# One-hots of slots laid out block by block in a two-stage mixture-of-experts kernel, and a second product taken by chunk halves

## What is computed

```python
x = x + _L0_ffn_ref(_L0_cond_ref(x, cond_8, ...), router_w, w1, b1, w2, b2)   # top 2 of 8 experts per token
x = x + _L1_ffn_ref(_L1_cond_ref(x, cond_8, ...), Wg, W1, b1, W2, b2)         # each expert takes its top 256 tokens
# _L1_ffn_ref:
G, I = jax.lax.top_k(S, k)                     # S: experts x tokens, k = 256
hid = gelu(einsum('ekh,ehf->ekf', xt[I], W1) + b1[:, None, :])
out = (einsum('ekf,efh->ekh', hid, W2) + b2[:, None, :]) * G[..., None]
new_x = zeros.at[I.reshape(-1)].add(out.reshape(-1, h))
```

## Time and profile before

| | before |
|---|---|
| median of 3 runs | 155.68 us (155.34 to 156.07) |
| span of the profiled execution | 153.7 us |
| median less span | 1.98 us |
| TensorE busy | 141.9 us (92%), 1100 matmuls |
| VectorE busy | 92.6 us (60%), 306 instructions |
| ScalarE busy | 82.2 us (53%) |
| GpSimd busy | 57.3 us (37%) |
| mean granted TensorE clock | 0.997 |

### The profile page before, as it was taken

How to read it: one execution, slowest core, us unless ns; L and a number is a source line. 1 busy time by engine, 2 the same in 40 slices (tenths; PEclk the granted TensorE clock), 3 DMA queues, 4 the chain that set the end, 5 groups by cost and what they waited for, 6 DMA issues and landing times.

```text
span 153.7 us, 3561 instructions
## 1 busy us (share of the span) xinstructions
PE 141.9 (92%) x1100; PEld 123.3 (80%) x1100; DVE 92.6 (60%) x306; ACT 82.2 (53%) x247; POOL 57.3 (37%) x62
## 2 busy tenths in 40 slices
PE   7999698899999999999799997979997999999990
PEld 3847687799999999964689975748986888889990
DVE  0278957756655555450599777765531685754872
ACT  0596807667777765620367769985126344445000
POOL 0000277344477554461500000002677777773000
PEclk9999999999999999999999999999999999999998
DMA  5994517999999972112702940040122221656634
GB/s 155 346 407 164 138 42 227 383 345 343 402 389 341 294 254 96 34 55 84 209 0 110 394 184 0 4 145 2 28 44 59 56 55 52 188 179 183 191 87 136
DMA packets 19252, 26.15 MB, mean 170 GB/s; under 512 B 1970, under 2 KB 13618, under 8 KB 18850
## 3 DMA queue, kind: packets, MB, share of 16 engines
q1 hardware_dynamic: 16386, 21.73, 41.6%
q0 software_dynamic: 1760, 3.67, 8.0%
q10 hardware_dynamic: 1088, 0.52, 1.2%
HBM read 19.98 MB, written 5.93 MB: 169 GB/s over the span
## 4 chain that ended last, share of the span: by engine, by line
PE 68%; DVE 15%; issue 5%; DMA 4%; POOL 4%; DVEq 1%; ACT 1%; POOLq 0%
PE bank L573 12%; PE bank L583 12%; PE bank L741 11%; PE bank L652 10%; PE bank L751 5%; POOL xg L445 3%; PE bank L475 3%; PE bank L619 3%; PE bank L628 2%; DMA xg<-rows,idx 2%; DVE y L1050 2%; DMA picked<-y,sidx 1%; DMA got<-picked 1%; DVE hid L1145 1%; PE bank L498 1%
## 5 line engine op out<-in xcount | busy, mean ns | idle before, releaser
L849 ACT ACTIVATE hT<-bank,w_now 128x128 f32<-128x128 f32 x92 | 26.3, 368 | 12.9 <-PE bank L573 12.9
L573 PE MATMUL bank<-xg,w_now 128*128 (+1 forms) x184 | 24.7, 277 | 1.3 <-ACT xg L842 0.8
L423 POOL DMA_INDIRECT xs<-rows,gidx x15 | 14.6, 976 | 28.6 <-DVE gidx L1057 17.9
L926 ACT ACTIVATE h1T<-bank,c_sb 128x256 f32<-128x256 f32 x44 | 18.2, 473 | 12.5 <-PE bank L652 12.5
L583 PE MATMUL bank<-w_sb,hT 128*128 (+1 forms) x184 | 24.4, 276 | 0.3 <-ACT hT L849 0.3
L573 PEld LDWEIGHTS bank<-xg,w_now 128*128 128x128 f32 x184 | 22.4, 192 | 2.4 <-issue 1.8
L583 PEld LDWEIGHTS bank<-w_sb,hT 128*128 128x128 f32 x184 | 22.4, 192 | 0.5 <-ACT hT L849 0.5
L741 PE MATMUL bank<-v_sb,h1T 128*128 128x128 f32 x176 | 22.7, 280 | 0.0
L741 PEld LDWEIGHTS bank<-v_sb,h1T 128*128 128x128 f32 x176 | 20.9, 192 | 1.4 <-ACT h1T L926 1.2
L428 POOL DMA_INDIRECT picked<-y,sidx x16 | 15.6, 977 | 10.3 <-DVE y L1106 9.1
L445 POOL DMA_INDIRECT xg<-rows,idx x14 | 14.0, 1000 | 5.7 <-issue 3.4
(11 more groups left out here) (201 smaller groups left out, 231.5 us busy)
## 6 DMA issues: line engine op xcount, KB each, us to landing
v_sb<-in_v SPq DMA_DIRECT2D x16, 256.0 KB
cw_sb<-in_cond_w SPq DMA_DIRECT2D x8, 386.5 KB, 5.4
plane<-y SPq DMA_DIRECT2D x5, 512.0 KB, 5.5
w_sb<-plane SPq DMA_DIRECT2D x5, 512.0 KB, 5.1
w_sb<-in_w SPq DMA_DIRECT2D x2, 1024.0 KB, 8.3
w_sb<-in_w SPq DMA_DIRECT2D x1, 1290.0 KB, 7.0
w_sb<-in_w SPq DMA_DIRECT2D x1, 774.0 KB, 4.9
rows<-row SPq DMA_DIRECT2D x1, 544.0 KB, 3.4
```

Source lines behind the costliest of these rows:

```text
L423: pool.indirect_dma_start(out=xs[:, b % RING], out_offset=None, in_=rows0, in_offset=rows_at(gidx, b)).then_inc(gathered[b % RING], 16)
L573: mm = pe.matmul(bank[2 + j % 2][:, P * f:P * f + P], w1_now[:, j % WB_RING, P * f:P * f + P], xsT[:, bass.ds((j - e) * P, P)], start=True ...
L849: ins = act.activation(hT[:, j % 2, P * f:P * f + P], bank[2 + j % 2][:, P * f:P * f + P], ACT.Relu, bias=w1_now[:, j % WB_RING, F + f:F + ...
L926: act.activation(h1T[:, n % 2, fc], bank[UP_BANKS[(2 * n + h) % 4]][:, CAP * f:CAP * f + CAP], ACT.Gelu, bias=c1_sb[:, e * NF + fc:e * NF ...
```

## The change

The one-hots of both stages are laid out block by block, `slot1h[i, s]` with the place s fastest. Each is made by one `tensor_scalar` compare per block of 128 tokens: the row of column numbers `iota` (128 bf16) against one float32 value per partition, read from a copy of the places (`locf`, `loc1f`). Stage one so has 16 compares of 128 elements in place of 2 of 1024, and each `place(e)` of stage two 8 in place of 1. `loc1` is now written in the order of its source. Both tables of repeated column numbers and the waits for them go. TensorE waits for the first-stage one-hots four at a time. A wait of VectorE for its own `hlf1h` is added ahead of `place`. For units 4 to 9 (six of the seven sparse experts) `down_e` gives way to `down_both`, which takes the hidden chunks 0 and 1 for both row halves first and then waits for the second half of the gelu and takes chunks 2 and 3; the last unit keeps `down_e`.

```diff
-        slot1h = sb("slot1h", [P, P, K * NC], BF16)
+        locf = sb("locf", [P, K * NC])
+        slot1h = sb("slot1h", [P, K * NC, P], BF16)
...
-        loc1 = sb("loc1", [P, E, NC], I16)
-
-        one1 = slot1h[:].rearrange("p s i -> p (s i)").rearrange("p (r s c) -> p r s c", r=2, c=NC)
+        loc1 = sb("loc1", [P, NC * E], I16)
+        loc1f = sb("loc1f", [P, NC, E])
+
+        one1 = slot1h[:].rearrange("p (r c) s -> p r c s", r=2)
...
             for i in range(K * NC):
-                pe.wait_ge(onehots, i // NC + 1)
-                mm = pe.matmul(bank[1][:, 0:2 * NB], slot1h[:, :, i], blkv[:, i].rearrange("p v b -> p (v b)"),
+                pe.wait_ge(onehots, i // 4 + 1)
+                mm = pe.matmul(bank[1][:, 0:2 * NB], slot1h[:, i], blkv[:, i].rearrange("p v b -> p (v b)"),
...
-                    mm = pe.matmul(bank[1][:, 0:2 * NH], one1[:, e % 2, :, c],
+                    mm = pe.matmul(bank[1][:, 0:2 * NH], one1[:, e % 2, c],
...
+            def down_both(n):
+                e = unit[n][1]
+                pe.wait_ge(h1T_ready, 4 * n + 2)
+                if n == HEAD:
+                    pe.wait_ge(yd_kept, HEAD)
+                if n == HEAD + 1:
+                    pe.wait_ge(idx1_ready, SPARSE)
+                for g in range(2):
+                    if g == 1:
+                        pe.wait_ge(h1T_ready, 4 * n + 4)
+                    for h in range(NH):
+                        if g == 0 and NH * (n - HEAD) + h >= 3:
+                            pe.wait_ge(y1_ready, NH * (n - HEAD) + h - 2)
+                        for f in (2 * g, 2 * g + 1):
+                            mm = pe.matmul(bank[y_bank(n, h)][:, C * h:C * h + C], h1T[:, n % 2, f, P * h:P * h + P],
+                                           v2_sb[:, e, f], start=(f == 0), stop=(f == NF - 1))
+                        if g == 1:
+                            mm.then_inc(y1_sent, 1)
...
-                for h in range(NH):
-                    down_e(n - 1, h)
+                down_both(n - 1)
...
-            act.activation(cols0, const("iota").unsqueeze(2).to_broadcast([P, P, K * NC]), ACT.Copy).then_inc(cols_ready, 1)
...
-            act.activation(cols1, const("iota").unsqueeze(2).to_broadcast([P, P, K * NC]), ACT.Copy).then_inc(cols_ready, 1)
...
+            v.tensor_copy(locf[:], loc[:])
...
-            v.wait_ge(cols_ready, 1)
-            for k in range(K):
-                v.tensor_tensor(slot1h[:, :, NC * k:NC * k + NC], cols0[:, :, NC * k:NC * k + NC],
-                                bc(loc[:, NC * k:NC * k + NC], 1, P), ALU.is_equal).then_inc(onehots, 1)
+            for i in range(K * NC):
+                ins = v.tensor_scalar(slot1h[:, i], iota[:], locf[:, i:i + 1], None, ALU.is_equal)
+                if i % 4 == 3:
+                    ins.then_inc(onehots, 1)
...
-            v.wait_ge(cols_ready, 2)
...
-            link(v.tensor_scalar(loc1[:].rearrange("p e c -> p c e"), posi[:].rearrange("p (c e) -> p c e", e=E), P - 1, None,
-                                 ALU.bitwise_and))
+            link(v.tensor_scalar(loc1[:], posi[:], P - 1, None, ALU.bitwise_and))
+            v.tensor_copy(loc1f[:].rearrange("p c e -> p (c e)"), loc1[:])
...
+            v.wait_ge(hlf1h_ready, 1)
+
             def place(e):
                 if e >= 2:
                     v.wait_ge(slots1, e - 1)
-                v.tensor_tensor(one1[:, e % 2], cols1[:, :, 0:NC], bc(loc1[:, e], 1, P),
-                                ALU.is_equal).then_inc(onehot1, 1)
+                for c in range(NC):
+                    ins = v.tensor_scalar(one1[:, e % 2, c], iota[:], loc1f[:, c, e:e + 1], None, ALU.is_equal)
+                ins.then_inc(onehot1, 1)
```

More of the change, by code:

```diff
@@ L215, in adaln_moe @@
         xa = bsc[:].rearrange("p (c d) -> p c d", c=NC)
-        cols0 = y0[:, 0:NC].rearrange("p c d -> p (c d)").bitcast(BF16).rearrange("p (s i) -> p s i", i=K * NC)
-        cols1 = xT_sb[:].bitcast(BF16).rearrange("p (s i) -> p s i", i=K * NC)
         pick0 = [y0[:, NC * (k + 1):NC * (k + 2)] for k in range(K)]
@@ L288, in adaln_moe @@
             "cr2_ready", "m1_ready", "m1s_ready", "g_ready", "gmat_ready", "logits"))
-        bsc_ready, w_summed, w_eff_ready, cols_ready = (sem(n) for n in (
-            "bsc_ready", "w_summed", "w_eff_ready", "cols_ready"))
+        bsc_ready, w_summed, w_eff_ready = (sem(n) for n in ("bsc_ready", "w_summed", "w_eff_ready"))
         pick0_ready = [sem("pick0_ready_0"), sem("pick0_ready_1")]
```

## The result

The changed kernel takes 159.06 us (median of 4 executions, 158.57 to 160.50) against 155.88 us for the kernel before in the same runs (155.34 to 156.09): ratio 1.0226 [1.0177, 1.0276], 2.3% slower. Two later comparisons gave 1.0199 [1.0154, 1.0244] and 1.0182 [1.0149, 1.0216]. The forecast was 157.1 us, so the sign was right and the size was not: +3.2 us where +1.4 was expected. The measured time lies inside the stated range, 155.8 to 159.2, at its upper edge. (Ratios leave disturbed executions out and the medians do not, so a ratio can differ a little from the quotient of its medians.)

What follows compares the result with a forecast made beforehand. VectorE alone was taken to bound the first stage, TensorE the second from 117.59, with the planes close behind. First stage +1.5 and second -0.1 made +1.4 us, hence 157.1 us; range 155.8 to 159.2.

Steps and rivals of the forecast that it cites:

- Price of one compare: On VectorE, a bf16 compare of 128 elements against a value per partition takes 0.165 us, bounds 0.10 and 0.20.
- Rivals 1 and 2: VectorE compares: at the bare rate, 0.10 us, 155.6 us in all, 12%; or no bf16 gain, 0.20 us, 159.1, 10%.
- first stage, +1.5 us, all of it on the chain: First stage: 16 compares and the copy to locf lengthen VectorE's queue by 1.5 us, none of it absorbed.
- The clock falls: TensorE, less busy from 15 to 19 us and between finds, drops to 1.2 GHz: 159 us, 7%.
- Rival 5: TensorE's clock falls to 1.2 GHz; the first block's 32 products cost up to 3.6 us more: 159 us, 7%.
- Rival 4: First stage: VectorE's wait before clearing y0 at 23.76 absorbs half of the shift: 156.3 us, 10%.
- Second stage: Places cost TensorE +0.6 us, down products give -0.8, so TensorE stands at -0.2; the end moves by about -0.1.
- The planes' 0.3 us of room: At the kernel's end, the planes on GpSimd's queue are only about 0.3 us from being the bound.
- Rival 3: Second stage: VectorE and GpSimd get in each other's way, planes come 1.3 us later than reckoned: 158.3 us, 13%.

Runs made afterwards that it cites:

- The probes: Kernel before with 24 compares of 128 bf16 elements and one of 1024 written to unused memory: 0.103 us against a constant, 0.163 against a value, 1.14 wide.
- warm-ups: Extra keep_warm products on TensorE ahead of the first block's 32 products; six in the changed kernel: 157.91 us, 1.0154; five in the kernel before: 156.11 us, 1.0006.
- the bare delay: Change's second stage on the kernel before, VectorE delayed 1.5 us by three wide compares, six keep_warm products added: 157.31 us, ratio 1.0069.
- the padded one: Change's second stage on the kernel before, first stage delayed 1.5 us by three wide compares into unused memory: 157.70 us, 1.0103; again 157.96 us, 1.0139.

## Why the prediction was right in sign and wrong in size

**Price of one compare: right.** 0.162 us, forecast 0.165. Rivals 1 and 2 fall with it. The probes show what the working only inferred: 0.103 us against a constant and 0.06 for the value. The Trainium skill (VectorE: DVE Perf Modes, the TRN2 errata), from which I had estimated 94 ns, is near the constant's form and has no term for the value; the measurement decides.

**The term that failed: "first stage, +1.5 us, all of it on the chain".** With the second stage of the change and without its first the ratio is 0.9977, with both 1.0199, on one chip: the term measured 3.5 us. It priced VectorE's time alone and put everything that follows from it at nothing. VectorE's own time was priced rightly. From the row of `psel` (12.39 before, 12.03 after) to the expert table it is 2.93 us before and 4.40 after, +1.47. With warm-ups the bare delay measured +1.4 us by the ratios. TensorE's sixteen products ran behind the compares four by four, as reckoned. Two of the things that follow are found, and a part stays open.

**First: "The clock falls", 7%.** The forecast gave the shift no consequence on TensorE. I had listed the fall as a rival and argued against it that no slice with gaps fell so far. That row is one execution, and it says what the clock did with TensorE busy for 1.63 us of that stretch. Counted from `psel`, the changed kernel has 1.04 us in a stretch of the same place and length (the 0.79 above is in part the earlier start). In all nine profiles of kernels with the longer first stage and no warm-up (the probes aside) the 32 products take 5.3 to 5.4 us, in the three with warm-ups 3.81. Yet the longer pause is not all of it. The profiles of the down products alone and of all of the second stage, with the first stage of the kernel before and the same 1.63 us of work in that stretch, have 5.44 us too, where five others with that first stage, two without and three with warm-ups, have 3.81. So the pause makes common what the kernel before does in some executions. The mean clock was .989 or lower in all 51 timed executions of kernels with the longer stretch and no warm-up, and in 34 of 90 of the kernel before; but the mean does not say in which stage it fell.

What it costs is less sure. At the turning of the fourth block of gathered rows (L557, 32.28 in the changed kernel, 20.25 us from `psel`) TensorE is 0.56 and 0.75 us earlier in the two profiles of the changed kernel with warm-ups, and 0.51 in the padded one. It is less than the 1.63 us that the products lengthen, since with the clock held TensorE waits for the gathered rows instead. At the kernel's end the only pair on one chip shows 0.5 us (1.0103 against 1.0069) with intervals that overlap, and the warm-ups in the kernel before gained nothing. I take 0.5 to 0.8 us; that it reaches the end in full is not shown. The warm-ups may not have held the clock in the first stage each time: two of four executions of the changed kernel and six of twelve of the padded one were at .989 or less, though the one of them that was profiled fell in the second stage. Rival 5 so named what happened, and gave 159 by a price of up to 3.6 us that it did not have; that it met the measured time is luck. So is that the range held: its upper edge stood for compares of 0.20 us.

Rival 4, the half absorbed shift, saw something real. VectorE waits 0.45 us less ahead of the clearing of y0, and with the clock held the fourth up product came only 1.18 us later, counted from `psel` (12.38 and 29.57). But the gathered rows, whose indices VectorE had written 1.48 us later, were not absorbed: TensorE waited for them next, and stood at +1.41.

**Second, a wait that was not in the sum: tau, +0.36 us.** It stands in all six profiles of kernels with both the sixteen and the eight-by-eight compares, and in none of those with one of the two or with wide ones. But such a wait does not need those compares. The kernel with the probes has neither set but 24 small compares of its own, 331 VectorE instructions in all, and a wait of about the same size a step earlier; from one such row to the next it takes 1.95 us there instead of 1.61:

```profile
109.62 0.16 DVE L1209 SCALAR_TENSOR_TENSOR enough<-count,signs 128x1 bf16<-128x1 f32 x1
110.03 0.16 DVE L1211 TENSOR_TENSOR ahead<-found,cst 128x1 f32<-128x1 f32 x1 [0.24 <-issue]
```

And the padded kernels wait 0.76 us ahead of their third weight copy where the others wait 0.31. So the place of such a wait moves with VectorE's instructions. What VectorE does in that time is not shown.

**Second stage: right.** From the first comparison with tau to TensorE's end it took 47.41 us before and 47.12 after, -0.29 for a forecast of -0.2. Find_slots is 0.35 us (0.40), a round 1.91 to 1.96 (1.98), the down product 1.78 (1.785), the first index +0.31 (+0.2), and turn_xg(2) +0.71 (+0.8), all counted from the same place. The copy to loc1f let the next instruction start after 0.11 us (0.09). One thing the forecast left out: the pauses between the finds can drop the clock as well. They did in four profiles with this second stage, none of them of the changed kernel itself, but TensorE took no longer there (47.2 to 47.5 us) than in the profiles without such a fall (47.1 to 48.2).

**The planes' 0.3 us of room: not borne out as a fixed bound.** In the first profile of the changed kernel the planes end 2.1 us after TensorE, in the second they end with it, in the third 2.1 before it. From the last scatter to the end of the last plane's addition it took 12.3, 10.2 and 9.4 us there, 11.0 in the kernel before and 8.8 in the one with the down products alone. That spread is larger than any of the shifts that the sum reckoned with. Rival 3 named a contention of VectorE and GpSimd, but of the new compares, and these did nothing (0.94 to 0.99 us beside them). What holds a transfer is one long VectorE instruction under which it starts, be it an addition of 1.22 us, a tensor_scalar of 0.75 or the old compare of 0.68. The change took the last of these away. The first gathers of the kernel before are 1.07 and 1.21 us long under it, and hlfv took 0.78 beside it against 0.47 now. The 1.02 us that I had read beside the tensor_scalars are the same thing, and no general slowing. The Trainium skill (SBUF — State Buffer, Who interferes with whom) says that a tensor_scalar in a two-port mode and a GpSimd instruction lock each other out for the whole instruction, and infers that tensor_tensor leaves the writing of descriptors alone. The rows agree with the first for the wide tensor_scalar (1.36 us); against the second they have 1.21, 1.65 and 1.82 us under tensor_tensors, and the measurement decides. Whether a transfer is caught for long hangs on the alignment: of three profiles of the changed kernel two have a pair over 1.6 us and one a single, and the kernel with all of the second stage and one of two identical padded kernels have none over 1.11.

**What stays open.** By the ratios, 155.8 us each: second stage -0.4, delay +1.4, clock +0.5 to +0.8, tau +0.4 make +1.9 to +2.2, and the changed kernel stood at +3.5, +3.1 and +2.8. Between 0.6 and 1.6 us are not accounted for. They seem to come with the sixteen instructions: for the kernel with two wide ones in their place the same sum, with a delay of 1.1 and no wait at tau, gives +1.2 to +1.5, and it measured +1.4. Single profiles show the rest in different places: in the first the planes' last landing (11.1 us from scatter to addition, 9.7 before), in the third a wait of 0.88 us for gathered rows at turn_xg. I have no row that ties either to the compares.

## What to carry to other kernels

Where a serial stretch of one engine grows, price also what the engine that waits for it does next: here 1.5 us of VectorE cost TensorE another 0.5 to 0.8 at its lower clock, and a row that shows the clock up in one execution says nothing of a longer pause, nor even of the next execution. Splitting one wide operation into sixteen small ones pays the fixed part sixteen times, and a per-partition value on top; a layout can be had with wide operations too, and should be tried that way first. And take a change's parts apart: this one holds a gain of 0.6% (`down_both`) under a loss of 2%.

## What was not expected of the hardware

A tensor_scalar of 128 bf16 elements costs 0.103 us with a constant and 0.163 with a value per partition, equally for a float32 and a bf16 value. Eight matmuls of 4 columns take 0.64 us with bf16 weights 16 elements apart and 0.35 with contiguous ones. A GpSimd transfer of 0.95 us that starts under a VectorE instruction of 1024 elements, with more than 0.13 us of it left, ends 0.81 to 0.84 us after it (84 of 84), so it takes up to 1.82. This holds for two-input additions (1.22 us), tensor_scalars (0.75) and bf16 compares of two tensors (0.68). And identical programs differed in the lower clock from one execution to the next: 34 of 90 executions of the kernel before were at .989 or less, with a median of 156.65 us against 155.72 for the others.
